# Cross-attention and routed-expert kernel: who waits for the output, one router-bias product per batch, an exponential placed ahead of the second batch

## The chip, the cores and the metric

The kernel runs on one core of one Trainium2 chip, whose engines are TensorE (PE in the profile; its weight loads PEld), VectorE (DVE), ScalarE (ACT), GpSimd (POOL) and SyncE (SP). An engine's own sequencer is PEq, ACTq and so on. The metric is the device time of one execution in microseconds (us); lower is better. All data is float32, and every number below is of this one core.

## The reference, cut to what matters

One Flamingo-style gated block on a batch of 2, with 512 tokens of 256 features each and 1024 context rows per batch:

```python
x = x + tanh(g_xattn) * xattn(layernorm(x), ctx, mask)      # 16 heads of 64, softmax over the visible keys
# routed feed-forward, on xf = layernorm(x)
logits = xf @ Wg + bg                                       # 8 experts
idx    = argmax(softmax(logits))
h      = gelu(xf @ W1[e] + b1[e]);  y = h @ W2[e] + b2[e]   # of the expert idx alone
x = x + tanh(g_ffn) * y[idx]
```

The mask is true for the hidden keys. With this data at most 160 keys are visible in each batch, and the kernel finds that window at run time.

## The kernel before, in words

The token tiles are 128 rows: tiles 0 to 3 (QT = 4) are batch 0, tiles 4 to 7 batch 1. Each engine has a program of its own, written out by hand; they meet at semaphores. Each program tests at run time whether one window of keys per batch suffices (`one_each`), and holds both forms of the rest: `rest(False)` for the window, which runs here, and `rest(True)` with more code. On SP, PE, ACT and DVE `rest(False)` is the If part, so at its end a branch jumps over the Else part; on POOL it is the Else part, and its end falls through. After that all engines meet at the end of the block; the profile puts those last instructions (DRAIN and EVENT_SEMAPHORE) on L136, and POOL collects the others' arrivals there.

**Order of the work.** Query projection and attention of batch 0; then, for each of the four tiles of batch 0, output projection (`project_tile`, L1551), residual and layer norm on DVE with a square root on ACT (`second_norm`, L1171; `std2`, L714), transposes on PE (`xn2_transposes`, L1565; copied out by ACT, `take_xt2`, L719) and the router's product (`tile_logits`, L1575). Those of the tiles 1 to 3 are interleaved with the start of batch 1's attention: context transposes, key projection in four groups (`attend_window`, L1634; `first_batch_logits`, L1856, puts the logits of the tiles 2 and 3 and the transposes of tile 3 between the groups), value projection (`project_v`, L1693), scores. Then DVE turns the logits into an expert and a place for each token (`route_logits`, L1096, to `route_place`, L1135, with `ranks`, L1584, on PE between), and POOL scatters the rows of the tiles to DRAM, sorted by expert (L581). SP reads them back (L454) one chunk of 128 rows per expert; batch 0's chunks go through the experts while the tiles 4 to 7 are projected, normalised and routed, batch 1's after them. Each expert result is scattered to the output by an indirect DMA that POOL issues (`put_out`, L594), 16 in all, each adding 16 to the semaphore `s_out`.

**The places that the change touches.**
- POOL's last wait, L691: `pool.wait_ge(s_out, 16 * B * E)`. SP's last waits are L523 and L524, for its own last two loads.
- `tile_logits`: for each tile two products of 128 rows with `wg_sb` (L1579), then one product with a single row, `ones` by the bias (L1580), all accumulated in 8 columns of `bank[5]` per tile. A float32 product shows as two MATMUL records, so L1579 stands with x4 and L1580 with x2. Only the last tile of a batch signals (`logit_ps`).
- ACT between the batches, L899 to L911: square roots for the four tiles, copies of the transposes and of the context, the last square root at L910; then `attend_window` (L790): two copies of key groups (L793), the copy of tile 3's transposes between them, a copy of the values (L796), and then the exponentials (`window_exp`, L773), whose first in batch 1 is preceded by an ACT_TABLE_LOAD that stands under the same line.
- DVE in the same stretch, L1285 to L1314: key copies, routing, `window_max` (L1249), `window_sum` (L1260, which waits for the exponentials of unit 0), copy of the values (L1293, which waits for the second value product), the places, and on.

Of the kernel before, what the change touches and what calls it, by code (L numbers as in the profile page):

```python
# [22 lines left out]
ACT = mybir.ActivationFunctionType  # L23
# [6 lines left out]
P = 128  # L30
# [66 lines left out]
def flamingo_kernel(nc, x, ctx_in, mask, g_xattn, g_ffn, wq, wk, wv, wo, bo, wg, bg, w1, b1, w2, b2, out):  # L97
# [38 lines left out]
    with ExitStack() as stack:  # L136
# [264 lines left out]
        @block.sync  # L401
        def _(sp):
            def load_x(b):
                sp.dma_start(x_sb[:, b * QT:(b + 1) * QT, :],
                             x[b].rearrange("(q p) d -> p q d", p=P)).then_inc(s_x[b], 16)

            def load_mask(b):
                sp.dma_start(mask_sb[:, b * QT:(b + 1) * QT, :],
                             mask[b].rearrange("(q p) k -> p q k", p=P)).then_inc(s_mask[b], 16)

            def load_wq(half):
                cols = slice(half * INNER // 2, (half + 1) * INNER // 2)
                sp.dma_start(wq_sb[:, :, cols], wq.rearrange("(c p) n -> p c n", p=P)[:, :, cols]).then_inc(s_wq[half], 16)

            for q in range(QT):
                sp.dma_start(x_sb[:, q, :], x[0, q * P:(q + 1) * P, :]).then_inc(s_x_tile[q], 16)
            load_wq(0)
            load_mask(0)
            load_wq(1)
            for b in range(1, B):  # L420
                load_mask(b)
                load_x(b)
            sp.dma_start(wk_sb[:], wk.rearrange("(c p) n -> p c n", p=P)).then_inc(s_wk, 16)
            sp.dma_start(wv_sb[:], wv.rearrange("(c p) n -> p c n", p=P)).then_inc(s_wv, 16)
            done = sp.alloc_register("sp_done")
            sp.reg_mov(done, 0)
            left = sp.alloc_register("sp_left")
            chunk = sp.alloc_register("sp_chunk")

            def load_ctx(b, slot, c):  # L430
                return sp.dma_start(ctx_sb[:, slot], ctx_in[b, bass.ds(c * CK, CK), :].rearrange("(t p) d -> p t d", p=P))

            def load_first_ctx():

                sp.wait_ge(visits_listed, 1)
                for b in range(B):
                    load_ctx(b, b, sp.value_load(visit[0:1, b, 1:2], min_val=0, max_val=NC - 1)).then_inc(s_first_ctx[b], 16)

            def load_window_ctx():

                for b in range(B):
                    w = sp.value_load(window[0:1, b:b + 1], min_val=0, max_val=NB - WB)
                    sp.dma_start(ctx_sb[:, b, 0, :], ctx_in[b, bass.ds(w * KB, WIDE), :]).then_inc(s_first_ctx[b], 16)
                    sp.dma_start(ctx_sb[0:LEFT, b, 1, :], ctx_in[b, bass.ds(w * KB + WIDE, LEFT), :])\
                        .then_inc(s_first_ctx[b], 16)

            chunk_rows = sorted_rows.rearrange("(e k p) r -> p e k r", e=E, p=P)

            def load_w2():
                sp.dma_start(w2_sb, w2.rearrange("e (c p) d -> p e c d", p=P)).then_inc(s_w2, 16)  # L450

            def read_rows(g, i, a, z):

                sp.dma_start(srow[g][:, a:z, :], chunk_rows[:, a:z, g, :]).then_inc(experts[g].s_rows[i], 16)  # L454

            def later_chunks(b):

                sp.reg_mov(left, sp.value_load(visit[0:1, b, 0:1], min_val=1, max_val=NC))
                sp.reg_add(left, left, -1)
                sp.wait_ge(first.ctxT_ps, b + 1)  # L460
                with sp.Fori(0, NC - 1) as i:
                    with sp.If(sp.snap(left) > 0):
                        n = sp.snap(done)
                        c = sp.value_load(visit[0:1, b, bass.ds(i + 2, 1)], min_val=0, max_val=NC - 1)

                        sp.wait_ge(later.ctxT_ps, n + 1)
                        load_ctx(b, b, c).then_inc(later.s_ctx, 16)
                        sp.reg_add(done, done, 1)
                        sp.reg_add(left, left, -1)
                    with sp.Else():  # L470
                        sp.nop()

            def rest(later_too):

                if later_too:
                    load_first_ctx()
                else:
                    load_window_ctx()
                sp.dma_start(wo_sb[:], wo.rearrange("(m p) d -> p m d", p=P)).then_inc(s_wo, 16)
                sp.dma_start(b2_sb[:], b2.unsqueeze(0).broadcast_to([P, E, D])).then_inc(s_b2, 16)  # L480
                sp.wait_ge(empty_ready, 2)
                sp.wait_ge(first.k_ps, KU)
                for k in range(CH):
                    sp.dma_start(chunk_rows[:, :, k, :], empty_row[:].unsqueeze(1).broadcast_to([P, E, RW]))\
                        .then_inc(s_empty, 16)
                if not later_too:
                    load_w2()
                for b in range(B):
                    if later_too:
                        later_chunks(b)  # L490
                    if b == 0:

                        sp.wait_ge(attn_done, 1)
                        sp.dma_start(w1_sb, w1.rearrange("e (c p) i -> p e c i", p=P)).then_inc(s_w1, 16)
                sp.wait_ge(s_sorted, 16 * QT)
                read_rows(0, 0, 0, E)
                if later_too:
                    sp.wait_ge(attn_done, B)
                    load_w2()
                sp.wait_ge(s_sorted, 16 * TT)  # L500
                for e in range(E):

                    if e >= 2:
                        sp.wait_ge(experts[1].s_rows[e - 2], 16)
                    read_rows(1, e, e, e + 1)
                sp.wait_ge(over_ready, 1)
                with sp.If(sp.value_load(over_any[0:1, 0:1], min_val=0, max_val=1) > 0):
                    sp.wait_ge(over_listed, 1)
                    used = sp.value_load(over_used[0:1, 0:1], min_val=0, max_val=NV)
                    for k in range(NV):  # L510
                        with sp.If(used > k):

                            if k > 0:
                                sp.wait_ge(experts[2].s_rows[0], 16 * k)
                            sp.reg_mov(chunk, sp.value_load(over_chunk[0:1, k:k + 1], min_val=0, max_val=E * CH - 1))
                            c = sp.snap(chunk, min_val=0, max_val=E * CH - 1)
                            sp.dma_start(srow[2][:, k, :], sorted_rows[bass.ds(c * P, P), :])\
                                .then_inc(experts[2].s_rows[0], 16)
                        with sp.Else():
                            sp.nop()  # L520
                with sp.Else():
                    sp.nop()
                for e in range(E - 2, E):  # L523
                    sp.wait_ge(experts[1].s_rows[e], 16)  # L524

            sp.wait_ge(visit_ready, 1)
            with sp.If(sp.value_load(one_each[0:1, 0:1], min_val=0, max_val=1) > 0):
                rest(False)
            with sp.Else():
                rest(True)  # L530

        @block.gpsimd
        def _(pool):
# [115 lines left out]
            def rest(later_too):  # L649
# [38 lines left out]
                            pool.nop()  # L688
                with pool.Else():
                    pool.nop()  # L690
                pool.wait_ge(s_out, 16 * B * E)  # L691

            chunk_expert = pool.alloc_register("pool_expert")
            pool.wait_ge(visit_ready, 1)
# [6 lines left out]
        def _(act):  # L701
# [185 lines left out]
            def rest(later_too):  # L887
# [10 lines left out]
                for b in range(B):  # L898
                    if b > 0:  # L899
                        std2(0)  # L900
                        std2(1)
                        take_xt2(0)
                        std2(2)
                        take_xt2(1)
                        if later_too:
                            take_ctxT(first, b)
                        else:
                            take_window_ctxT(b)
                        take_xt2(2)
                        std2(QT - 1)  # L910
                    also = no_fill if b == 0 else first_batch_xt2  # L911
                    if later_too:
                        attend(first, b, b, (negm_run, l_run), (lambda k: take_q(1, 2 * k)) if b == 0 else no_fill, also)
# [601 lines left out]
        def _(pe):  # L1515
# [59 lines left out]
            def tile_logits(tt):  # L1575
                pe.wait_ge(xt2_sb, tt + 1)
                at = slice((tt % QT) * E, (tt % QT + 1) * E)
                for c in range(DC):
                    nc.tensor.matmul(bank[5][:, at], xnT[:, c, tt * P:(tt + 1) * P], wg_sb[:, c, :], start=(c == 0), stop=False)  # L1579
                last = nc.tensor.matmul(bank[5][:, at], ones[0:1, :], bg_sb[0:1, :], start=False, stop=True)  # L1580
                if tt % QT == QT - 1:
                    last.then_inc(logit_ps, 1)

# [518 lines left out]
```

## Time and profile before, and how to read it

| | us |
|---|---|
| median of 3 runs (210.47 to 210.69) | 210.49 |
| span of the profiled execution | 216.8 |
| PE busy in the span | 196.8 (91%) |
| DVE, ACT, POOL busy | 125.5, 105.5, 89.5 |

The profiled execution is one of its own: its span goes from the first to the last instruction, and the profile gives no other time for it. It is 6.3 us longer than the median of the timed runs. In a timeline row the first number is the start, the second how long the row's instructions took together, x8 how many they are, and a bracket at the end the idle time ahead of them and who ended it. PE's matrix products are pipelined and their ends are modelled, so the start of the next row tells better than a duration when PE went on. Rows by line give the shortest, the median and the longest in ns, and the starts of the first and the last.

### The profile page before, as it was taken

Reading aid. Unit: us, or ns where it says so; the run is one execution under the profiler, and the core shown is the slowest. Engines: PE = TensorE matmul, PEld = TensorE weight load, DVE = VectorE, ACT = ScalarE, POOL = GpSimd, SP = SyncE. Lnnn points to the kernel's source line nnn. Section 1 sums busy time; section 2 is a strip of 40 time slices with the busy share of each in tenths; the row PEclk is TensorE's granted clock in tenths of the full one; section 3 lists DMA queues with packets and bytes.
Section 4 is the critical chain, followed back from the end, with each engine's and each line's share of the span. In section 5 each row is a group of like instructions: output and inputs, shape, how many; then the busy total and the mean of one; then the engine's idle time right before and its main releaser. Section 6 shows DMA issues by size and latency. Waiting matters only on the chain.

```text
span 216.8 us, 3994 instructions
## 1 busy us (share of the span) xinstructions
PE 196.8 (91%) x1262; PEld 144.4 (67%) x1262; DVE 125.5 (58%) x526; ACT 105.5 (49%) x377; POOL 89.5 (41%) x129
## 2 busy tenths in 40 slices
PE   7899899799999999999997999989999996399940
PEld 7644576567765546888956667758889994289930
DVE  3896755998893321443279999887343450145420
ACT  3232618799994213022187999976312451135410
POOL 7000632577579600000007997689100057433460
PEclk9999999999999999999999999999999999559995
DMA  5993589999998001900000106000000014520011
GB/s 135 348 385 129 173 315 323 307 287 300 236 216 266 6 0 38 347 1 0 5 0 25 52 26 196 5 0 3 2 0 0 0 52 128 145 72 17 31 52 21
DMA packets 21505, 25.16 MB, mean 116 GB/s; under 512 B 1939, under 2 KB 19805, under 8 KB 21344
## 3 DMA queue, kind: packets, MB, share of 16 engines
q1 hardware_dynamic: 19456, 22.51, 35.2%
q0 software_dynamic: 1152, 2.12, 2.9%
q8 instruction: 13, 0.21, 0.5%
q10 hardware_dynamic: 864, 0.15, 0.4%
q14 instruction: 20, 0.16, 0.3%
HBM read 14.14 MB, written 11.68 MB: 119 GB/s over the span
## 4 chain that ended last, share of the span: by engine, by line
PE 78%; DVE 8%; ACT 5%; issue 4%; DMA 1%; POOL 1%; POOLq 0%; DVEq 0%; ACTq 0%
PE s_bank L1606 13%; PE o_bank L1561 13%; PE s_bank L1906 7%; PE o_bank L1689 7%; PE o_bank L1917 7%; PE t_bank L1663 7%; PE s_bank L1646 6%; PE s_bank L1715 4%; ACT probs L779 4%; PE o_bank L1682 4%; PE s_bank L1895 2%; PE t_bank L1697 2%; DVE probs L1249 1%; PE t_bank L1579 1%; DVE pT L1270 1%
## 5 line engine op out<-in xcount | busy, mean ns | idle before, releaser
L617 POOL TENSOR_TENSOR probs<-probs,r_col 128x512 f32<-128x512 f32 x32 | 33.4, 1043 | 62.1 <-DVE r_col L1260 61.7
L779 ACT ACTIVATE probs<-probs,negm_run 128x160 f32<-128x160 f32 x128 | 53.0, 416 | 5.1 <-DVE negm_run L1249 5.0
L1249 DVE CUSTOM_DVE_ANT_0 probs<-s_bank,maskneg 128x160 f32<-128x160 f32 x128 | 33.2, 318 | 5.8 <-PE s_bank L1646 5.6
L1606 PE MATMUL s_bank<-xnT,wq_sb 128*128 128x512 f32 x64 | 28.8, 598 | 0.5 <-ACT xnT L728 0.5
L1561 PE MATMUL o_bank<-wo_sb,oT 128*128 128x256 f32 x128 | 28.6, 379 | 0.0
L1561 PEld LDWEIGHTS o_bank<-wo_sb,oT 128*128 128x128 f32 x128 | 23.9, 190 | 3.5 <-issue 0.5
L779 ACT ACTIVATION_READ_ACCUMULATOR probs<-probs,negm_run 128x1 f32 x128 | 24.0, 187 | 0.0
L596 POOL DMA_INDIRECT out_dram<-oT x16 | 15.9, 996 | 15.8 <-DVE oT L1198 13.4
L1646 PE MATMUL s_bank<-k_sb,q_sb 64*128 64x160 f32 x256 | 22.3, 311 | 0.0
L1646 PEld LDWEIGHTS s_bank<-k_sb,q_sb 64*128 64x128 f32 x256 | 17.9, 186 | 4.8 <-issue 4.0
L1606 PEld LDWEIGHTS s_bank<-xnT,wq_sb 128*128 128x128 f32 x64 | 11.7, 190 | 13.6 <-issue 13.5
L1917 PE MATMUL o_bank<-oT,k_sb 128*128 128x256 f32 x64 | 17.6, 401 | 3.2 <-issue 3.2
L1198 DVE SCALAR_TENSOR_TENSOR oT<-o_bank,gate,oT 128x256 f32<-128x256 f32 x16 | 7.6, 482 | 22.0 <-PE o_bank L1917 17.6
L1663 PE MATMUL t_bank<-ident,probs 128*128 128x128 f32 x128 | 18.7, 284 | 1.7 <-issue 1.1
L1663 PEld LDWEIGHTS t_bank<-ident,probs 128*128 128x128 f32 x128 | 13.5, 141 | 8.7 <-issue 6.3
L1906 PE MATMUL s_bank<-k_sb,q_sb 128*128 128x128 f32 x128 | 18.8, 294 | 0.0
L581 POOL DMA_INDIRECT sorted_rows<-rows,place x8 | 8.0, 1006 | 24.0 <-DVE place L1142 22.2
L1906 PEld LDWEIGHTS s_bank<-k_sb,q_sb 128*128 128x128 f32 x128 | 17.3, 208 | 0.9 <-ACT k_sb L872 0.4
L1689 PE MATMUL o_bank<-pT,v_sb 128*64 128x256 f32 x128 | 17.5, 393 | 0.0
L881 ACT ACTIVATE k_sb<-s_bank,b1T 128x128 f32<-128x128 f32 x32 | 10.0, 364 | 14.1 <-PE s_bank L1906 9.4
L1917 PEld LDWEIGHTS o_bank<-oT,k_sb 128*128 128x128 f32 x64 | 11.4, 199 | 5.0 <-issue 3.8
L739 ACT COPY q_sb<-s_bank 128x512 f32<-128x512 f32 x10 | 5.8, 584 | 16.5 <-PE s_bank L1606 16.5
(155 smaller groups left out, 296.8 us busy)
## 6 DMA issues: line engine op xcount, KB each, us to landing
sorted_rows<-empty_row SPq DMA_DIRECT2D x8, 1040.0 KB, 14.9
oT<-in_L_ffn_W_dram SPq DMA_DIRECT2D x1, 2048.0 KB, 20.0
q_sb<-in_L_ffn_W_dram SPq DMA_DIRECT2D x1, 2048.0 KB, 8.3
oT<-sorted_rows SPq DMA_DIRECT2D x1, 1040.0 KB, 5.4
oT<-sorted_rows SPq DMA_DIRECT2D x8, 130.0 KB, 2.0
wq_sb<-in_L_xattn_Wq_dram SPq DMA_DIRECT2D x2, 512.0 KB, 6.1
mask_sb<-in_mask_BxSxS_bk_dram SPq DMA_DIRECT2D x2, 512.0 KB, 7.1
wk_sb<-in_L_xattn_Wk_dram SPq DMA_DIRECT2D x1, 1024.0 KB, 11.0
```

What stands on the lines that cost most here:

```text
L596: nc.gpsimd.indirect_dma_start(out=out_rows, in_=srow[g][:, p, 0:D], in_offset=None, out_offset=bass.IndirectOffsetOnAxis(ap=srow[g][:, p, ...
L617: nc.gpsimd.tensor_tensor(window_wide(u), window_wide(u), r.rearrange("p i h -> p (i h)") .unsqueeze(2).broadcast_to([P, 4, WIDE]), ALU.mu ...
L779: last = nc.scalar.activation(window_part(u, i, h), window_part(u, i, h), ACT.Exp, bias=negm_run[at], scale=-1.0, accum_out=l_run[at])
L881: last = nc.scalar.activation(hT[:, p % 2, at], hT_bank(p)[:, at], ACT.Gelu, bias=bias(ic))
L1249: nc.vector.tensor_tensor_reduce(window_part(u, i, h), s_bank[u % 2][:, h, i * CK:i * CK + WK], maskneg[:, q, 0:WK], -SCALE, LARGEST, ALU. ...
L1561: last = nc.tensor.matmul(bank[6 + tt % 2][:, 0:D], oT[:, b, m, q * P:(q + 1) * P], wo_sb[:, m, :], start=(m == 0), stop=(m == M - 1))
L1606: last = nc.tensor.matmul(bank[m % 4], wq_sb[:, c, m * P:(m + 1) * P], xnT[:, c, b * N:(b + 1) * N], start=(c == 0), stop=(c == DC - 1))
L1646: last = nc.tensor.matmul(s_bank[u % 2][:, h, i * CK:i * CK + WK], q_sb[head_rows[h], b, m, q * P:(q + 1) * P], k_sb[head_rows[h], m, 0:WK ...
L1663: last = nc.tensor.transpose(bank[4 + a][:, h * HALF + i * P:h * HALF + (i + 1) * P], window_wide(u)[:, 2 * i + h, :], ident[:])
L1689: last = nc.tensor.matmul(o_bank[head_rows[h], a, 0:HALF], v_sb[:, 0, at * DH:(at + 1) * DH], wide_pT[:, a, h, :], start=False, stop=True)
L1906: last = nc.tensor.matmul(hT_bank(e)[:, ic * P:(ic + 1) * P], w1_sb[:, e, c, ic * P:(ic + 1) * P], sxT[:, e % 2, c * P:(c + 1) * P], start ...
L1917: last = nc.tensor.matmul(bank[6 + p % 2][:, 0:D], hT[:, p % 2, ic * P:(ic + 1) * P], weights(ic), start=(ic == 0), stop=(ic == IC - 1))
```

## The change

SP, as its last statement of `rest`, waits until all 16 results have landed, and POOL no longer does. The bias is multiplied once per batch, for all four tiles at once (32 columns, from a broadcast access pattern), ahead of the first tile's products, and no longer once per tile behind them. ACT does one exponential of a constant (`warm[:]`, a scratch column) behind the last square root of batch 0's tiles.

```diff
@@ SP, rest()
                 for e in range(E - 2, E):
                     sp.wait_ge(experts[1].s_rows[e], 16)
+                sp.wait_ge(s_out, 16 * B * E)
@@ POOL, rest()
-                pool.wait_ge(s_out, 16 * B * E)
@@ ACT, rest()
                         take_xt2(2)
                         std2(QT - 1)
+                        nc.scalar.activation(warm[:], eps[:], ACT.Exp)
@@ PE, tile_logits(tt)
+                if tt % QT == 0:
+                    nc.tensor.matmul(bank[5][:, 0:QT * E].rearrange("p (t e) -> p t e", e=E), ones[0:1, :],
+                                     bg_sb[0:1, :].unsqueeze(1).broadcast_to([1, QT, E]), start=True, stop=False)
                 for c in range(DC):
-                    nc.tensor.matmul(bank[5][:, at], xnT[:, c, tt * P:(tt + 1) * P], wg_sb[:, c, :], start=(c == 0), stop=False)
-                last = nc.tensor.matmul(bank[5][:, at], ones[0:1, :], bg_sb[0:1, :], start=False, stop=True)
+                    last = nc.tensor.matmul(bank[5][:, at], xnT[:, c, tt * P:(tt + 1) * P], wg_sb[:, c, :], start=False,
+                                            stop=(tt % QT == QT - 1 and c == DC - 1))
```

## Rows read from the trace of the kernel before

**Rows 1.** Page, chain that ended last: share of the span by engine.
```profile
PE 78%; DVE 8%; ACT 5%; issue 4%; DMA 1%; POOL 1%; POOLq 0%; DVEq 0%; ACTq 0%
```

**Rows 2.** Timeline of PE, 104 to 113 us: start, us, engine, line, operation.
```profile
104.39 1.25 PE L1715 MATMUL s_bank<-ctxT,wk_sb 128*128 128x160 f32 x8
105.48 0.51 PE L1579 MATMUL t_bank<-wg_sb,xnT 128*128 128x8 f32 x4
105.92 0.38 PE L1580 MATMUL t_bank<-bg_sb,ones 1*128 1x8 f32 x2
106.23 1.35 PE L1715 MATMUL s_bank<-ctxT,wk_sb 128*128 128x160 f32 x8
107.42 1.88 PE L1697 MATMUL t_bank<-wv_sb,ctxT 128*128 128x512 f32 x4
...
112.88 1.07 PE L1702 MATMUL o_bank<-wv_sb,ctxT 128*32 128x256 f32 x16
```

**Rows 3.** Timeline of ACT, 101 to 112 us; brackets: idle before, and its releaser.
```profile
101.61 0.30 ACT L716 ACTIVATE std<-rows,eps 128x1 f32<-128x1 f32 x1
102.43 0.42 ACT L793 COPY k_sb<-s_bank 128x320 f32<-128x320 f32 x1 [0.52 <-PE s_bank L1715]
104.59 0.37 ACT L721 COPY xnT<-t_bank 128x256 f32<-128x256 f32 x1 [1.74 <-PE t_bank L1571]
...
109.94 1.28 ACT L779 ACT_TABLE_LOAD   x1
111.24 0.43 ACT L779 ACTIVATE probs<-probs,negm_run 128x160 f32<-128x160 f32 x1
```

**Rows 4.** Timeline of DVE, 110 to 114 us.
```profile
110.20 0.33 DVE L1249 CUSTOM_DVE_ANT_0 probs<-s_bank,maskneg 128x160 f32<-128x160 f32 x1 [0.23 <-PE s_bank L1646]
...
113.09 0.18 DVE L1260 RECIPROCAL r_col<-l_run 128x4 f32<-128x4 f32 x1 [0.69 <-ACT probs L779]
113.19 0.66 DVE L1293 COPY v_sb<-o_bank 128x512 f32<-128x512 f32 x1
```

**Rows 5.** Timeline of PE, 168 to 171 us.
```profile
168.94 0.44 PE L1571 MATMUL t_bank<-ident,wq_sb 128*128 128x128 f32 x2
...
170.09 0.51 PE L1579 MATMUL t_bank<-wg_sb,xnT 128*128 128x8 f32 x4
170.52 0.38 PE L1580 MATMUL t_bank<-bg_sb,ones 1*128 1x8 f32 x2
170.84 1.16 PE L1906 MATMUL s_bank<-k_sb,q_sb 128*128 128x128 f32 x8
```

**Rows 6.** Timeline of DVE and of ACT, 168 to 170 us.
```profile
168.30 0.41 DVE L998 TENSOR_SCALAR wq_sb<-rows 128x256 f32<-128x256 f32 x1
...
168.08 1.28 ACT L932 ACT_TABLE_LOAD   x1
...
169.48 0.35 ACT L721 COPY xnT<-t_bank 128x256 f32<-128x256 f32 x1
```

**Rows 7.** Waits: engine, line, releaser: us in total, times, longest.
```profile
POOL sorted_rows L581 <- DVE place L1142: 22.2, 1, 22.2
```

**Rows 8.** Instructions of single lines: ns min/median/max, first and last start in us.
```profile
L697 POOLq COMPARE_BRANCH  x1: 37/37/37, 214.3 to 214.3; - x1
...
L136 POOLq DRAIN  x1: 2040/2040/2040, 214.5 to 214.5; - x1
...
L527 SPq COMPARE_BRANCH  x2: 38/44/49, 20.2 to 191.4; - x2
...
L136 SPq DRAIN  x1: 58/58/58, 192.9 to 192.9; - x1
...
L1503 DVEq COMPARE_BRANCH  x1: 47/47/47, 210.1 to 210.1; - x1
...
L136 DVEq DRAIN  x1: 66/66/66, 214.8 to 214.8; - x1
...
L2068 PEldq COMPARE_BRANCH  x1: 5425/5425/5425, 208.6 to 208.6; - x1
```
## The prediction, made before the change was run

> **What bounds the kernel now.** I read the chain of waits first: 78% of the span is PE's own work [rows 1], so a PE instruction that goes away where PE is the chain is worth its time, up to the next engine that is late. Then I read the three places that the diff touches: batch 1's start around 100 to 114 us, batch 1's routing around 168 to 171 us, and the end. In the first two the reader is to see which engine each start waits for; in the last, what stands between the landing of the last result and the end. A measurement of this kernel can tell about 0.2% (0.4 us) from no change.
>
> **Place 1, batch 1's start.** Three of the four bias products of batch 0 go; tile 0's stays, wider and earlier.
> - One costs 0.31 us on PE, from its start at 105.92 to the next start at 106.23. The key group behind it takes 107.42 - 106.23 = 1.19, while a group of the same eight products behind transposes takes 105.48 - 104.39 = 1.09 [rows 2]: 0.10 more. So tile 1's is worth 0.31 and those of the tiles 2 and 3, each ahead of a key group, 0.41: 1.13 us sooner for all that PE does behind the key groups.
> - The wide product has 32 columns in place of 8, which no row shows for one row of weights. The nearest rows bound it: not under zero more, and, if its time grew with the columns, 4 times 0.31, so at most 0.93 more [rows 2]. I take nothing: the four products of 128 rows with the same 8 columns take 105.92 - 105.48 = 0.44 together, 0.11 each, and eight with 160 columns 1.09, 0.14 each [rows 2], so columns of this number hardly count. Both ends go into the range.
> - The exponential's table load takes 1.28 us at 109.94, ahead of the first exponential at 111.24 [rows 3]. In its new place it begins behind the square root of 101.61, about 101.9, and with an activation of 0.3 us as that one is it ends at about 103.5. Queued behind it is the key copy that now starts at 102.43; it comes about 1.1 us late. Its cover: the next ACT copy stands at 104.59 after 1.74 idle [rows 3], and the scores, which wait for the key copies, come behind the first value product of 107.42 [rows 2]. So it costs nothing. Without that cover it would cost at most its own 1.6 us.
> - What is late next: DVE's copy of the values at 113.19. It stands behind a reciprocal that waited 0.69 us for the exponentials [rows 4], and itself needs PE's second value product, done at 112.88 [rows 2]. After the change PE is there at 112.88 - 1.13 = 111.75. The exponentials: DVE's maxima start when PE's scores are there (its idle 0.23 before 110.20 was ended by them [rows 4]), so at 109.07; the first exponential can then start at about 109.7, and unit 0 takes the 1.85 us from 111.24 to 113.09 [rows 3, 4], to about 111.5. So the copy starts at about 111.8, held by PE, in place of 113.19: **1.39 us**. The load's move alone would give 113.19 - 112.93 = 0.26, the bias alone 1.13. If the reciprocal were the only bound it would be 1.6 or 1.7, the upper end; the lower end is 0, if the late key copy binds. From there DVE, POOL and PE hand each other the same order of work, and PE's chain runs on to the projection of tile 4, so I carry the 1.39 on whole.
>
> **Place 2, batch 1's routing.** The biases of the tiles 5 and 6 go ahead of the last transposes (168.94), 0.62 us, and tile 7's behind them.
> - The transposes need the norm of tile 7, done at 168.30 + 0.41 = 168.71 [rows 6]. The square root ahead of it waits for DVE's variance, a chain that starts at tile 7's projection, which no removed product precedes; a copy on ACT ahead of it gets out of its way, for which I count under 0.1. So PE, ready at 168.32, waits until about 168.65: 0.29 gained of 0.62.
> - The products of tile 7, at 170.09 [rows 5], could then start at 169.80. They need ACT's copy, which ends at 169.48 + 0.35 = 169.83 behind the Gelu's table load of 168.08 [rows 6], so that load is level with PE: the next bound.
> - Tile 7's bias, 170.84 - 170.52 = 0.32 [rows 5], stood between those products and DVE's routing. It goes. Sum **0.61 us**. Ends: 0.3 (the last product alone) and 0.93 (all three).
> - What follows: POOL waits idle for the places (22.2 us in one wait [rows 7]) and then scatters, SP reads back, batch 1's expert chunks start. PE's work ahead of them moves by as much. I carry the 0.61 to the end.
>
> **Place 3, the end.** Now the last result lands at about 214.3, when POOL's branch is released; POOL's DRAIN starts at 214.5 and takes 2.04, to 216.54; the other engines are there before [rows 8]. After the change POOL's DRAIN can start when its last issue is done, some three us sooner. If it takes 2.04 then too, it is covered. SP's wait ends on its branch, with nothing queued behind it but that branch and its own DRAIN. Now the branch starts at 191.4 and the DRAIN behind it at 192.9 [rows 8]: 1.5 us. So SP arrives at 214.3 + 1.5 + 0.06 = 215.86, in place of 216.54: **0.7 us**. DVE, at 214.8, would be next [rows 8], so the upper end is 1.7. The lower end comes from the other engines' jumps over their untaken halves: DVE needs from 210.1 to 214.8, 4.7 us, and PE's branch 5.4 [rows 8]; with those SP would arrive 2.5 or 3.2 us later than POOL does now. I take SP's own row, since code and engine are the same. The Trainium skill (Runtime: NRT & Kernel Launch, Instruction fetch mechanics) speaks against this place: a taken branch whose target is outside the fetched window makes the engine fetch it before going on, so what is put ahead of such a branch at the very end exposes a fetch that was hidden. By that rule the trace agrees, with three branches of 1.5, 4.7 and 5.4 us.
>
> **The sum.** 1.39 + 0.61 + 0.7 = 2.7 us. The profiled execution spans 216.8, 6.3 more than the median; its sum gives 214.1. I do not know where its 6.3 us lie, and none of the terms rests on them, so I take 2.7 from the median: 210.49 - 2.7 = **207.8 us**.
>
> **The rivals.**
> 1. *SP's jump at the end.* Its branch costs more than SP's row says. It loses against now from 2.2 us on, and against all that the places 1 and 2 give (2.0) from 4.2 us on. At DVE's 4.7 the time is 210.49 - 2.0 + 2.5 = 211.0, at PE's 5.4 it is 211.7: slower than before. For it: two engines of three. Against it: SP's own row, and that at 214 us the transfers are over. Chance 0.07 for slower, 0.05 for a branch near 4.2 that evens it out, 0.07 for one between 2.2 and 3.7 that leaves 208.5 to 210.
> 2. *POOL's DRAIN ends last all the same*, because it takes its 2.04 us from the last landing, whoever waits. No row shows it at another place behind indirect transfers. Then place 3 gives nothing: 208.5. Chance 0.16.
> 3. *SP's branch is short*, because SP has stood there for 20 us and what lies behind is loaded. DVE is next: 1.7 in place of 0.7, 206.8. Chance 0.12.
> 4. *Place 1 gives nothing*: the load, moved ahead of the key copy, is paid there, or the first exponential still loads, so that the change doesn't do there what it says, and the bias's time is lost in a wait for ACT. 210.49 - 1.3 = 209.2. Chance 0.07.
>
> **How the numbers follow.** The forecast has 0.46. Faster: 0.46 + 0.16 + 0.12 + 0.07 + 0.07 = 0.88; same 0.05; slower 0.07. The range reaches down to 206.4, all three upper ends (1.7 + 0.93 + 1.7) nearly, and up to 209.3, rival 4 and a wide product at its dear end; it leaves out rival 1's upper cases.
>
> **What would show it.** Right: two L1580 pairs in place of eight, no ACT_TABLE_LOAD between the value copy and the first exponential, DVE's value copy 1.4 us closer to the key groups; the routing's first reduction about 0.6 us closer to tile 7's projection, with PE waiting ahead of the last transposes; POOL's DRAIN starting before the last landing, and SP's DRAIN about 1.5 us behind it. Wrong: a SP branch of 4 us, a POOL DRAIN that ends 2 us behind the landing, scores that wait for ACT's key copy, or a wide product that takes over 1 us.

## The result, and the profile after

The changed kernel takes **207.88 us** (207.69 to 208.14) where the kernel before takes 210.48 beside it: a ratio of 0.9877, 95% interval 0.9865 to 0.989, so 2.60 us less (2.3 to 2.8). The forecast was 207.8.

The profile of before that stands ahead of the prediction spans 216.8 us, and was disturbed: PE stood 3.2 us at 182 us, and its granted clock then lay at the 1.2 GHz level (0.5 of 2.4) until about 195. A second profile of the same kernel (the first experiment) spans 208.7, in line with its timed runs; the comparisons below are made with that one, "before again". The profiled execution of after spans 205.9 and took 207.76 in all, so a time is a span and 1.86.

**The page.** Busy time of PE, and the chain that ended last by engine. PE was busy 196.8 us in the disturbed profile and 192.9 in before again; now it is 191.5, and the chain is PE's own work as before [rows 1].

```profile
PE 191.5 (93%) x1250; PEld 139.1 (68%) x1250; DVE 125.5 (61%) x526; ACT 105.7 (51%) x378; POOL 89.5 (43%) x129
...
PE 80%; DVE 9%; ACT 4%; issue 2%; DMA 1%; POOL 1%; POOLq 0%; DVEq 0%; ACTq 0%
```

**Place 1.** Timeline of PE, 94 to 115 us; these rows answer to [rows 2].

```profile
94.84 0.40 PE L1580 MATMUL t_bank<-bg_sb,ones 1*128 1x32 f32 x2
95.17 0.61 PE L1583 MATMUL t_bank<-wg_sb,xnT 128*128 128x8 f32 x4
...
104.84 0.51 PE L1583 MATMUL t_bank<-wg_sb,xnT 128*128 128x8 f32 x4
...
106.37 1.88 PE L1701 MATMUL t_bank<-wv_sb,ctxT 128*128 128x512 f32 x4
...
111.83 1.07 PE L1706 MATMUL o_bank<-wv_sb,ctxT 128*32 128x256 f32 x16
```

No single-row product stands behind tile 3's router product (104.84) any more, and the first value product starts at 106.37, not 107.42. Timelines of ACT and of DVE, which answer to [rows 3, 4]:

```profile
101.66 1.28 ACT L911 ACT_TABLE_LOAD   x1
102.95 0.20 ACT L911 ACTIVATE warm<-eps 128x1 f32<-128x1 f32 x1
103.06 0.41 ACT L793 COPY k_sb<-s_bank 128x320 f32<-128x320 f32 x1
103.95 0.37 ACT L721 COPY xnT<-t_bank 128x256 f32<-128x256 f32 x1 [0.48 <-PE t_bank L1572]
...
109.76 0.43 ACT L779 ACTIVATE probs<-probs,negm_run 128x160 f32<-128x160 f32 x1 [0.89 <-DVE negm_run L1250]
```

```profile
111.62 0.18 DVE L1261 RECIPROCAL r_col<-l_run 128x4 f32<-128x4 f32 x1 [0.27 <-ACT probs L779]
111.94 0.69 DVE L1294 COPY v_sb<-o_bank 128x512 f32<-128x512 f32 x1
112.54 0.42 DVE L1139 TENSOR_TENSOR place_e<-earlier,rank 128x32 f32<-128x32 f32 x1
```

The load now lies behind the square root. The key copy behind it is 0.63 us late and nobody waits for it: the next copy still has 0.48 idle ahead of it. The first exponential waits for DVE and not for a table, and DVE's copy of the values starts at 111.94 in place of 113.19, no longer right behind the reciprocal: it waits for PE's second value product, which is the next bound that the prediction named. What comes behind does not go by that copy, though: see the exponential alone, below.

**Place 2.** Timeline of PE, 156 to 169 us, which answers to [rows 5].

```profile
156.44 3.62 PE L1562 MATMUL o_bank<-wo_sb,oT 128*128 128x256 f32 x16
159.99 0.40 PE L1580 MATMUL t_bank<-bg_sb,ones 1*128 1x32 f32 x2
160.32 0.61 PE L1583 MATMUL t_bank<-wg_sb,xnT 128*128 128x8 f32 x4
160.79 0.41 PE L1572 MATMUL t_bank<-ident,wq_sb 128*128 128x128 f32 x2
...
161.47 3.62 PE L1562 MATMUL o_bank<-wo_sb,oT 128*128 128x256 f32 x16
...
167.32 0.44 PE L1572 MATMUL t_bank<-ident,wq_sb 128*128 128x128 f32 x2 [0.38 <-DVE wq_sb L999]
...
168.47 0.60 PE L1583 MATMUL t_bank<-wg_sb,xnT 128*128 128x8 f32 x4
```

PE now waits 0.38 us for tile 7's norm ahead of the last transposes, as forecast. But the wide product stands ahead of tile 7's projection (161.47), on which that norm hangs. POOL's long wait for the places is 21.9 us in place of 22.2 [rows 7]. The routing's first reduction on DVE, in before again and in after:

```profile
170.97 0.19 DVE L1102 TENSOR_REDUCE lmax<-t_bank 128x4 f32<-128x32 f32 x1 [2.30 <-PE t_bank L1580]
```

```profile
169.17 0.19 DVE L1103 TENSOR_REDUCE lmax<-t_bank 128x4 f32<-128x32 f32 x1 [1.90 <-PE t_bank L1583]
```

**Place 3.** Instructions of single lines at the end, which answer to [rows 8]: durations in ns, then the starts.

```profile
L525 SPq EVENT_SEMAPHORE  x1: 28/28/28, 204.7 to 204.7; - x1
...
L528 SPq COMPARE_BRANCH  x2: 38/44/49, 20.2 to 204.8; - x2
...
L136 POOLq DRAIN  x1: 4617/4617/4617, 201.1 to 201.1; - x1
...
L136 DVEq DRAIN  x1: 66/66/66, 205.1 to 205.1; - x1
L136 SPq DRAIN  x1: 59/59/59, 205.2 to 205.2; - x1
```

SP is released by the landing at 204.65, branches, and is in its DRAIN at 205.18: 0.42 us from branch to DRAIN, not 1.5. POOL's DRAIN starts early, at 201.06, and takes 4.62 instead of 2.04: it ends at 205.68, 1.03 behind the landing and 0.44 after SP's, so POOL still ends last.

### The profile page after: what moved, and what is told of

Same layout as the page of the kernel before. It is cut to its first block, busy times and chain, and to the rows that moved or that the text cites. A ratio compares the mean times of both kernels' runs of the same rounds, so it can differ in the third digit from the quotient of the medians.

```text
span 205.9 us, 3970 instructions
## 1 busy us (share of the span) xinstructions
PE 191.5 (93%) x1250; PEld 139.1 (68%) x1250; DVE 125.5 (61%) x526; ACT 105.7 (51%) x378; POOL 89.5 (43%) x129
## 4 chain that ended last, share of the span: by engine, by line
PE 80%; DVE 9%; ACT 4%; issue 2%; DMA 1%; POOL 1%; POOLq 0%; DVEq 0%; ACTq 0%
PE s_bank L1610 14%; PE o_bank L1562 13%; PE o_bank L1693 7%; PE s_bank L1650 7%; PE t_bank L1667 7%; PE s_bank L1910 6%; PE o_bank L1921 6%; PE s_bank L1719 4%; PE o_bank L1686 4%; ACT probs L779 3%; PE s_bank L1899 2%; PE t_bank L1701 2%; DVE probs L1250 2%; DMA rows<-in_x_dram 1%; DVE pT L1271 1%
## 5 line engine op out<-in xcount | busy, mean ns | idle before, releaser
L582 POOL DMA_INDIRECT sorted_rows<-rows,place x8 | 8.0, 1005 | 23.6 <-DVE place L1143 21.9
L1910 PE MATMUL s_bank<-k_sb,q_sb 128*128 128x128 f32 x128 | 17.2, 277 | 0.1
L1921 PE MATMUL o_bank<-oT,k_sb 128*128 128x256 f32 x64 | 16.4, 383 | 0.0
L1910 PEld LDWEIGHTS s_bank<-k_sb,q_sb 128*128 128x128 f32 x128 | 15.7, 192 | 0.9 <-issue 0.4
L1175 DVE SCALAR_TENSOR_TENSOR rows<-o_bank,gate,rows 128x256 f32<-128x256 f32 x8 | 3.9, 484 | 17.0 <-PE o_bank L1562 17.0
```

Of the source, the lines that this page charges most:

```text
L1910: last = nc.tensor.matmul(hT_bank(e)[:, ic * P:(ic + 1) * P], w1_sb[:, e, c, ic * P:(ic + 1) * P], sxT[:, e % 2, c * P:(c + 1) * P], start ...
L1921: last = nc.tensor.matmul(bank[6 + p % 2][:, 0:D], hT[:, p % 2, ic * P:(ic + 1) * P], weights(ic), start=(ic == 0), stop=(ic == IC - 1))
```

## Experiments

Where the time went, in distances that a late or early start doesn't touch, from the timelines of all kernels (us). *Place 1*: from the first projection of batch 0 to that of batch 1. *Place 2*: from there to the routing's first reduction. *Landing*: of the last result, from the span's start. *End*: from the landing to the last instruction. The ratio is to the kernel before on the same chip.

| kernel | time | ratio, 95% interval | place 1 | place 2 | landing | end |
|---|---|---|---|---|---|---|
| before again | 210.81 | 1.0004, 0.9991 to 1.0016 | 66.63 | 20.24 | 206.25 | 2.47 |
| wait alone | 209.71 | 0.9947, 0.9927 to 0.9967 | 66.64 | 20.24 | 206.99 | 1.27 |
| bias alone | 208.98 | 0.9927, 0.991 to 0.9944 | 65.57 | 19.86 | 204.63 | 2.47 |
| exponential alone | 210.28 | 0.998, 0.9968 to 0.9992 | 66.21 | 20.24 | 206.29 | 2.47 |
| bias and exponential | 209.03 | 0.9917, 0.9897 to 0.9938 | 65.13 | 19.86 | 204.32 | 2.47 |
| after, POOL waits too | 208.85 | 0.9912, 0.9891 to 0.9933 | 65.14 | 19.86 | 204.31 | 2.47 |
| **after** | 207.88 | 0.9877, 0.9865 to 0.989 | 65.14 | 19.86 | 204.65 | 1.27 |
| after again | 207.66 | 0.9849, 0.9831 to 0.9868 | 65.15 | 19.86 | 204.66 | 1.27 |
| after, ACT waits | 209.55 | 0.9931, 0.9909 to 0.9954 | 65.15 | 19.86 | 204.65 | 3.57 |
| after, no far jump at the end | 208.35 | 0.9881, 0.9847 to 0.9915 | 65.15 | 19.86 | 204.90 | 1.27 |
| after, two engines without it | 207.76 | 0.9857, 0.9837 to 0.9878 | 65.14 | 19.86 | 204.43 | 1.27 |
| after, late bias | 207.17 | 0.9821, 0.9795 to 0.9846 | 65.13 | 19.33 | 204.05 | 1.27 |

**The kernel before, again.** No edit.

> The kernel before, profiled once more. The profile of it that the prediction used spanned 216.8 us, 6.3 more than the timed median, and PE stood for 3.2 us at 182 to 185 us and ran on at half clock until about 195. Theory: that stretch was a disturbance of that one execution, and a usual one spans about 208.6 (the changed kernel's span of 205.9 lies 1.9 under its time), with the places at 110 to 114 and 168 to 171 us as before and an end of 2.2 us between the last landing and the end of POOL's DRAIN. Rival: the stretch belongs to the kernel before and the change removed it; then the span is again near 216 and PE stands for some 3 us.

The span is 208.7 and the time that of before, so what the prediction could not place was that one profile's: 8.1 us of span, seen as 6.3 because a time is 1.86 longer than its span. The end is as it was read from [rows 8], with one difference. Single lines of SP and of POOL:

```profile
L507 SPq COMPARE_BRANCH  x1: 50/50/50, 189.2 to 189.2; - x1
...
L527 SPq COMPARE_BRANCH  x2: 38/44/49, 20.2 to 191.9; - x2
...
L136 SPq DRAIN  x1: 58/58/58, 192.3 to 192.3; - x1
...
L136 POOLq DRAIN  x1: 2040/2040/2040, 206.4 to 206.4; - x1
```

SP needs 0.42 us from the branch of L527 to its DRAIN here, where it had stood 2.7 us since its branch before that (L507).

**The wait alone**, on the kernel before:

```diff
+                sp.wait_ge(s_out, 16 * B * E)
...
-                pool.wait_ge(s_out, 16 * B * E)
```

> Only the wait for the output moves from POOL to SP. Theory (POOL's DRAIN starts early and then ends about 1.0 us behind the last landing, SP's branch is short because SP has stood at the wait): 1.0 to 1.2 us faster than before, about 209.4, POOL's DRAIN of over 4 us, SP's branch to its DRAIN 0.4 us. Rival, the prediction's term (SP's branch takes 1.5 us and ends last): 209.8. Rival, POOL's DRAIN ends 2 us behind the landing whoever waits: 210.5.

0.96 us less by the medians, 1.1 by the ratio, with the places 1 and 2 untouched. POOL's DRAIN and SP's wait:

```profile
L136 POOLq DRAIN  x1: 4660/4660/4660, 203.4 to 203.4; - x1
...
L525 SPq EVENT_SEMAPHORE  x1: 28/28/28, 207.0 to 207.0; - x1
```

The DRAIN ends at 208.02, 1.03 behind the landing at 206.99, and again it is the last.

**The bias alone**, on the kernel before:

```diff
+                if tt % QT == 0:
...
-                last = nc.tensor.matmul(bank[5][:, at], ones[0:1, :], bg_sb[0:1, :], start=False, stop=True)
```

> Only the bias product is made once per batch; the exponential's table load stays ahead of the first exponential, and POOL waits. Theory: 1.05 us from batch 1's start, all of it passed on because the load moves with the value copy ahead of it, and 0.4 from batch 1's routing, about 209.0. Rival (what the bias frees at batch 1's start is lost in a wait for ACT's load, so that bias and load only pay together): 0.4, 210.1.

1.06 at place 1 and 0.38 at place 2, 1.5 us by the ratio and 1.7 by the medians. The same run says what SP's 1.5 us of [rows 8] were. SP's branches and its DRAIN:

```profile
L507 SPq COMPARE_BRANCH  x1: 50/50/50, 188.0 to 188.0; - x1
...
L527 SPq COMPARE_BRANCH  x2: 38/44/49, 20.2 to 189.5; - x2
...
L136 SPq DRAIN  x1: 58/58/58, 190.7 to 190.7; - x1
```

Here the second branch comes 1.5 us after the first, and the DRAIN 1.2 after that: 2.7 from L507's branch to the DRAIN. It is 2.6 in bias and exponential and 2.7 in the kernel where ACT waits, and was 2.8 in the first profile. Only where SP stood 2.7 us or longer between the two did the second cost 0.42. So the 1.5 us was the rest of what L507's branch had started, and not the price of the branch of L527.

**The exponential alone**, on the kernel before:

```diff
+                        nc.scalar.activation(warm[:], eps[:], ACT.Exp)
```

> Only the early exponential. Theory: DVE's value copy then waits for PE's second value product instead of the exponentials, so 0.26 us, plus up to 0.25 because the place arithmetic on DVE no longer runs beside POOL's first product: 210.0 to 210.2. Rival (the key copy that the load pushes back is waited for): 210.5 or more. Rival (the load's 1.28 us all come off): 209.2.

0.42 at place 1, nothing elsewhere; the time says 0.4. DVE's copy of the values starts only 0.2 us sooner, but the reciprocal and POOL's first product behind it come 0.4 sooner, and `place_e` takes 0.43 in place of 0.68. Timelines of DVE and POOL in before again:

```profile
113.05 0.18 DVE L1260 RECIPROCAL r_col<-l_run 128x4 f32<-128x4 f32 x1 [0.69 <-ACT probs L779]
...
113.72 0.68 DVE L1138 TENSOR_TENSOR place_e<-earlier,rank 128x32 f32<-128x32 f32 x1
...
113.31 1.04 POOL L617 TENSOR_TENSOR probs<-probs,r_col 128x512 f32<-128x512 f32 x1 [39.61 <-DVE r_col L1260]
```

and with the exponential alone:

```profile
112.64 0.18 DVE L1261 RECIPROCAL r_col<-l_run 128x4 f32<-128x4 f32 x1 [0.28 <-ACT probs L779]
112.95 0.69 DVE L1294 COPY v_sb<-o_bank 128x512 f32<-128x512 f32 x1
113.56 0.43 DVE L1139 TENSOR_TENSOR place_e<-earlier,rank 128x32 f32<-128x32 f32 x1
...
112.90 1.04 POOL L617 TENSOR_TENSOR probs<-probs,r_col 128x512 f32<-128x512 f32 x1 [39.19 <-DVE r_col L1261]
```

`place_e` ends 0.05 us behind POOL's product here (113.99 behind 113.94), in before again (114.40 behind 114.35), and in every other profile of the record; in batch 1's routing, where POOL stands idle, the same instruction takes 0.19. So its end goes with POOL's product, which starts on the reciprocal, and not with the copy of the values ahead of it. The distances say the same: from this reciprocal to batch 1's first projection it is 37.68 to 37.70 us in all profiles, from the copy 37.59 in before again and 37.37 in after. What the load's move gains is thus how much sooner the exponentials begin, 0.42 of the load's 1.28. No run moved POOL's product by itself.

**Bias and exponential**, the change without the wait (after, with its wait line put back on POOL):

> The bias product once per batch and the early exponential, POOL waiting for the output as before. Theory (the two add up at batch 1's start: 1.06 from the bias, 0.41 from the load as the runs of one part alone showed, and 0.35 from batch 1's routing): 1.8 us faster than before, 208.8 beside 210.6, and the changed kernel beats it by the end's 0.8 to 1.0. Rival (the bias makes the exponentials later or earlier than DVE's value copy, so that the load is worth more behind the bias than alone): 2.2 us or more.

1.50 at place 1 (1.06 + 0.42 = 1.48 from the two alone) and 0.38 at place 2: they add up. What is left to after, 0.88 in the spans (206.80 to 205.92) and 0.8 in the ratios, is the wait's.

**Both wait**, after with one line more:

```diff
+                pool.wait_ge(s_out, 16 * B * E)
```

> The changed kernel, but POOL waits for the output as well as SP. Theory (POOL's DRAIN takes 2.04 us from where it starts, if it starts behind the landing, and ends 1.0 us behind the landing if it started before it): the end is as in the kernel before, 2.2 us from the landing to the end of the DRAIN, 0.8 to 1.2 us slower than the changed kernel, so 1.6 to 1.8 us faster than before. Rival (SP's standing at the wait, not POOL's early DRAIN, is what gains): as the changed kernel, 2.6 us faster than before.

The time is that of bias and exponential. SP is out of the way early and the gain of the wait is gone, since POOL's DRAIN starts behind the landing again. Single lines of the end:

```profile
L525 SPq EVENT_SEMAPHORE  x1: 28/28/28, 204.3 to 204.3; - x1
...
L136 POOLq DRAIN  x1: 2040/2040/2040, 204.5 to 204.5; - x1
...
L136 SPq DRAIN  x1: 59/59/59, 204.8 to 204.8; - x1
```

So the wait's gain is that POOL is in its DRAIN when the result lands; that SP waits is only the place where the wait does no harm.

**ACT waits** instead of SP:

```diff
-                sp.wait_ge(s_out, 16 * B * E)
...
+                act.wait_ge(s_out, 16 * B * E)
```

> The changed kernel, but ACT waits for the output instead of SP. ACT's branch over its other half takes 3.7 to 4.4 us to its DRAIN in the kernels so far, where it does not stand before it. Theory 1 (a branch at which the engine has stood is short, because the fetch behind it goes on while it stands, as SP's 0.4 us in place of 1.5 suggests): ACT's branch takes under 1 us and the time is that of the changed kernel, 2.6 us faster than before. Theory 2 (the fetch starts only when the branch is taken, and SP's was short because its target is near): ACT arrives 3.7 us or more behind the landing, 2.5 to 3.2 us slower than the changed kernel, level with before or slower.

Slower than after by 1.1 us in the ratios, and by 2.3 in the profile, which is the slowest of its six runs. That speaks against theory 1, and is less than theory 2 said. ACT's branch at the end of its If part, and the DRAINs of POOL and ACT:

```profile
L969 ACTq COMPARE_BRANCH  x2: 38/44/49, 23.1 to 204.7; - x2
...
L136 POOLq DRAIN  x1: 4300/4300/4300, 201.4 to 201.4; - x1
...
L136 ACTq DRAIN  x1: 81/81/81, 207.9 to 207.9; - x1
```

ACT had stood at its wait for 6 us, and still needs 3.24 us from its branch to its DRAIN. Standing there is not enough, then. That the time goes into a fetch that begins when the branch is taken is the reading that fits; no row names the engine of a fetch. Both branches jump over an Else part, and SP's has less code in it than ACT's. The Trainium skill (Runtime: NRT & Kernel Launch, Instruction fetch mechanics) states that a taken branch forces a fetch only where its target lies outside the window of pages already held; by that rule the trace agrees, with 0.42 on SP and 3.24 on ACT, each behind the last landing. That SP's target lies in that window, no run here shows. Rival 1 of the prediction is thus real, on another engine.

**No far jump at the end.** The last landing comes 4.1 us behind its issue in after, where the median of the 16 output transfers is 2.7. In this kernel the two forms are exchanged on PE, ACT and DVE, so that the ends of the form that runs fall through:

```diff
-            with act.If(one > 0):
-                rest(False)
+            with act.If(many > 0):
+                rest(True)
             with act.Else():
-                rest(True)
+                rest(False)
...
```

> The changed kernel with the two forms of the rest exchanged on PE, ACT and DVE: the form that runs is the Else part, so that these engines fall through at the end and jump over the other form at about 20 to 25 us instead. The last output takes 3.8 to 4.2 us from its issue to its last landing, the ones before it 2.0; the last ones fall together with the instruction fetches of PE's, ACT's and DVE's jumps. Theory (those fetches hold up the landing): the last landing comes 1 to 2 us sooner, and the jumps at 20 to 25 us hide behind PE's queue of query products: 1 to 2 us faster than the changed kernel. Rival 1 (the landing's tail is POOL's own descriptors): no gain at the end. Rival 2 (PE's early jump, 5 us long, is paid at 24 us): 1 to 3 us slower.

The last landing is 2.67 us behind its issue (202.23 to 204.90), and yet the time is that of after: the theory's landing came, its gain in time did not. SP's wait, the last output issue, and PE where it waits for batch 1's first chunk:

```profile
L525 SPq EVENT_SEMAPHORE  x1: 28/28/28, 204.9 to 204.9; - x1
...
L597 POOL DMA_INDIRECT out_dram<-oT x16: 983/985/1216, 178.6 to 202.2; - x16
```

```profile
183.60 0.75 PE L1899 MATMUL s_bank<-ident,xnT 128*128 128x128 f32 x4 [2.03 <-DVE xnT L1184]
```

What was won at the end was lost ahead of it: batch 0's first projection starts at 84.66 in place of 84.17, and PE waits 2.03 us for batch 1's first chunk where it waits 0.97 in after. Beside that second wait the trace shows one 16 KB instruction transfer while SP's read of the chunk is under way; in after that transfer lies 9 us earlier. That the one delays the other was not tried by itself.

**Two engines without it**: the same exchange on ACT and DVE, PE left as in after.

> The kernel after, with the two forms of the rest exchanged on ACT and DVE alone, so that their ends fall through and fetch nothing late; PE keeps its order, its long branch near the end and its fetches between the stages. Theory 1, that all late fetches together hold up the last result's landing (4.1 us from its issue in the kernel after, 2.7 where PE, ACT and DVE fetched nothing late): the landing comes 0.3 to 1.0 us sooner, since two of three such fetches are gone, and POOL's DRAIN ends 1.03 us behind it: 206.9 to 207.6 us. Theory 2, that PE's fetch alone holds it up: the landing stays at about 4.0 us from its issue and the time at 207.9. Under both, the early jumps of ACT and DVE at about 20 us may cost up to 0.5 us where PE waits for them, which shows in the first projection behind batch 0's attention, at 84.2 now.

No gain: the landing is 3.38 us behind its issue (after again, on the same chip: 3.72), and batch 0's first projection starts at 84.78 in place of 84.19. So the early loss belongs to ACT's and DVE's early jumps, not to PE's. Theory 1 holds in its sign (4.1 and 3.7 with all far jumps at the end, 3.4 without two, 2.7 without any), but the time it promised did not come: with the early loss of 0.6 the span is 0.2 shorter than that of after again (205.70, 205.93) and the time no shorter (207.76, 207.66).

**After again**, on that chip:

> The kernel after, unchanged, beside the run before it on the same chip: 207.7 to 208.1 us, a ratio of about 0.9877 to the kernel before, the last landing 4.0 to 4.2 us behind its issue, POOL's DRAIN ending 1.03 us behind that landing and last of all.

207.66, 0.9849 of before (0.9831 to 0.9868), so a little under the first result and overlapping it at its end. The DRAIN takes 4.21 us and ends 1.04 behind the landing.

**Late bias.** After, with batch 1's bias moved out of the way of tile 7's projection:

```diff
-                if tt % QT == 0:
...
+                if tt == 0:
+                    bias(0, QT, True)
                 for c in range(DC):
...
+                if tt == TT - 2:
+                    bias(0, QT - 1, False)
+                    bias(QT - 1, QT, False)
```

> The kernel after, but batch 1's bias is no longer ahead of tile 7's projection: it is multiplied as two products (24 columns and 8 columns) behind tile 6's router products, where PE waits 0.38 us for tile 7's norm. Theory 1, that place 2 gave only about 0.38 instead of 0.61 because the wide product costs 0.41 to 0.43 us on PE ahead of the projection that the norm hangs on: tile 7's projection begins 11.75 us behind the first projection of batch 1 (12.16 in the kernel after), the last transposes find PE late by itself again, 0.2 us sooner than in the kernel after and with no wait for the norm, and the routing's first reduction comes 19.65 us behind the first projection (19.86 after, 20.24 before). Time 207.5 to 207.8. Theory 2, that the routing in the kernel after is held by ACT's Gelu table load whatever PE does: the reduction stays at 19.85 or comes later, with PE's last router products waiting for ACT's copy.

Theory 1 holds, and by more than it said: the routing's first reduction comes 0.53 sooner, not 0.21. Tile 7's projection begins 11.64 us behind batch 1's first one, where 11.75 was expected. Timelines of PE and of DVE:

```profile
156.45 3.62 PE L1562 MATMUL o_bank<-wo_sb,oT 128*128 128x256 f32 x16
159.90 0.51 PE L1585 MATMUL t_bank<-wg_sb,xnT 128*128 128x8 f32 x4
160.27 0.42 PE L1572 MATMUL t_bank<-ident,wq_sb 128*128 128x128 f32 x2
...
166.36 0.61 PE L1580 MATMUL t_bank<-bg_sb,ones 1*128 1x24 f32 x4
166.90 0.44 PE L1572 MATMUL t_bank<-ident,wq_sb 128*128 128x128 f32 x2
```

```profile
168.65 0.19 DVE L1103 TENSOR_REDUCE lmax<-t_bank 128x4 f32<-128x32 f32 x1 [1.91 <-PE t_bank L1585]
```

Without the wide product the projections and the router's product behind them take 160.27 - 156.45 = 3.82 us to the transposes, with it 160.79 - 156.44 = 4.35: the wide product costs 0.53 there, of which 0.33 is its own, 0.10 lies in the group ahead and 0.10 in the product behind. Moved, it takes 0.54 us as two products (166.36 to 166.90), most of which falls into the time that PE waited for the norm (0.38 in after). At 207.17 us this is the fastest kernel here. It was not run on one chip with after: the intervals of its ratio (0.9795 to 0.9846) and of after again's (0.9831 to 0.9868) overlap, it lies below that of after's first result, and its profile ends 0.6 us sooner than after's, of which 0.53 is this place.

## Why the prediction was right, and where not

The total was right (207.88 for 207.8), the sum of three terms of which one was a little small, one too large, and the third about right for a wrong reason; that their errors nearly cancel is luck. In the spans they measure 1.49 + 0.38 + 0.88 = 2.75; the times say 2.60.

- **Place 1, 1.39 forecast, 1.49 measured, by another path.** What was told came: PE is sooner by the bias, the load is out of the exponentials' way, the key copy's lateness is covered, the value copy is held by PE (111.94 for "about 111.8"). The step that failed is that this copy sets what follows ("I carry the 1.39 on whole"). Counted from batch 0's first projection, the copy came 1.27 sooner (29.04 to 27.77), the reciprocal 1.50 (28.95 to 27.45), and batch 1's first projection went with the reciprocal, over POOL's product. The prediction had that bound as its upper end, "1.6 or 1.7"; so the nearness of 1.39 is partly luck. Alone, the bias gives 1.06 (1.13 forecast) and the load's move 0.42 (0.26 forecast, which was the copy's). "I take nothing" for the wide product was nearly right: from tile 2's projection to tile 3's, with tile 0's router product between them, it is 4.60 us (91.29 to 95.89) where before again has 4.49, so 0.11 more.
- **Place 2, 0.61 forecast, 0.38 measured.** The step that failed is "a chain that starts at tile 7's projection, which no removed product precedes", together with "I take nothing". Nothing was gained ahead of that projection, and the wide product, which took the place of tile 4's small one there, is dearer: the projection starts 12.16 us behind batch 1's first projection where it started 12.05. The norm is 0.11 later by that, PE waits for it (0.38), and of "0.29 gained" at the transposes 0.17 is left (18.01 behind batch 1's first projection, 18.18 in before again). The other half, "0.32" for tile 7's bias, measured 0.22: from that tile's router product to the reduction it is 0.70 where it was 0.92. The late bias shows the price of the wide product's position: with the biases in PE's wait the place gives 20.24 - 19.33 = 0.91.
- **Place 3, 0.7 forecast, 0.88 measured (0.8 to 1.1 by the times).** SP's own row was not the price of its branch: 0.42, not 1.5. And the DRAIN that was to be covered is the last to end: not 2.04 behind the landing (rival 2's price) but 1.03, the same in after, after again, the wait alone and the four other kernels in which POOL does not wait, within 0.01 us, whether it had started 2.1 or 3.6 us ahead of the landing. From the landing to the end is thus 1.27 for 2.47, a gain of 1.20. About 0.33 of that was given back before it: the landing itself is at 204.65 in after and at 204.31 and 204.32 in the two kernels with the same work in which POOL waits.
- **That last 0.33 stays open.** From the routing's first reduction to the landing it is 35.1 to 35.7 us in the five kernels where POOL waits, and 35.45 to 35.93 in the four others that keep all jumps and the order of work; the scatter is as large as the difference. In after the 0.33 shows between the last issue and the landing (4.12 us beside 3.73 and 3.76); in after again that is 3.72, and the issue is later instead. That POOL's early DRAIN delays the landing was not tried by itself.
- **The rivals.** 1 falls on SP and holds on ACT. 2 is right that POOL's DRAIN ends last and wrong in its price. 3 is right that SP's branch is short, but its reason, that SP has stood there, is not shown (ACT stood too), and DVE is not next: its DRAIN ended at 205.17, half a us ahead of POOL's. 4 falls.

## What to carry to other kernels

Put a wait for the last result on an engine whose way from there to the program's end is short, and let the engines with much to do at the end (a DRAIN behind indirect transfers, a jump over much code) do it while the transfer is under way; then read all engines' ends against the landing, not against each other. Before a duration is taken as an instruction's price, look at what its engine did shortly before: here it was the rest of an earlier jump. When small products are gathered into one, ask what hangs on the work behind the place where they are gathered: the same product cost half a microsecond ahead of the projection that the routing hangs on, and fell mostly into a wait a few microseconds later. And where two rows could each hold what follows, take the distance from each to a later event in several kernels: the one whose distance stays the same is on the path.

## What the runs showed of the hardware that was not expected

- POOL's DRAIN behind indirect transfers took 2.04 us when it began after the last landing, and ended 1.03 to 1.04 behind the landing when it began 2.1 to 3.6 us ahead of it, taking 3.2 to 4.7.
- A one-row product costs about 0.3 us whether it has 8, 24 or 32 columns (0.31 to 0.33 from its start to the next start, 0.27 each for two in a row), and some 0.1 more in each of its neighbours.
- Far jumps at the end go with a late last landing: 3.7 to 4.2 us behind its issue with them, 3.4 in the one kernel without two of them, 2.7 in the one without any. ACT's and DVE's jumps early in the program cost 0.5 to 0.6.
- DVE's `place_e`, a TENSOR_TENSOR of 32 columns, took 0.19 us with POOL idle and 0.42 to 0.68 beside POOL's TENSOR_TENSOR of 512 columns, ending 0.05 behind it whenever it had begun.
- The table load took 1.28 us and the next activation began at 102.95, the moment the load was over. The Trainium skill (ScalarE: Activation LUTs, What ACT_TABLE_LOAD costs) adds a DRAIN of about 1.38 us to each load, 2.66 in all; this trace differs, since none stands there and the key copy follows at 103.06.
